# Post-layernorm transformer layer on 8 cores: the projection's cast moves from GpSimd to ScalarE, and the layer-norm finish is queued one group earlier

## The reference

```python
q = (x @ q_w.T + q_b).reshape(b, s, 16, 128)
k = x @ k_w.T + k_b
v = x @ v_w.T + v_b
scores = einsum('bqhd,bkd->bhqk', q, k) / 128 ** 0.5      # causal mask, softmax
out = einsum('bhqk,bkd->bqhd', attn, v).reshape(b, s, 2048)
x = _layernorm(x + out @ o_w.T + o_b)
x = _layernorm(x + einsum('bsi,oi->bso', x, weight * scale_weight[:, None]) + bias)
# _layernorm: (x - mean) / sqrt(var + 1e-5)
```

## Time and profile before

| what | us |
|---|---|
| runs shown: median (lowest, highest) of 2 | 2372.36 (2342.03, 2402.69) |
| profiled execution, its own time | 2288.15 |
| its span, slowest core (core 3) | 2286.6 |
| spans of the eight cores | 2271.2 to 2286.6 |
| closing stage in that span | 1538.8 to 2286.6 |

### The profile page before, as it was taken

The page is one execution under the profiler, slowest core; times in us unless marked ns, Lnnn a source line. Parts: engine busy times, 40 slices in busy tenths (PEclk is TensorE's granted clock), DMA queues, the critical chain, the costliest instruction groups (busy, mean ns, idle before and its releaser), DMA issues.

```text
span 2286.6 us, 26159 instructions; the slowest of 8 cores (2271.2 to 2286.6 us)
## 1 busy us (share of the span) xinstructions
PE 1545.0 (68%) x7216; PEld 671.9 (29%) x7216; DVE 919.3 (40%) x1985; ACT 906.9 (40%) x2270; POOL 384.0 (17%) x399
## 2 busy tenths in 40 slices
PE   0899963445555566666566666669879595989773
PEld 0344421222222222222223332333323232333221
DVE  0000003445555555555555555540626415166234
ACT  0112114655555565666555555551123320123311
POOL 0000020000000000000000000007646244675331
PEclk9999985666766667777577677679989798999886
DMA  9222289800000000000000000006543346553252
GB/s 146 39 38 43 41 101 110 112 1 1 1 1 1 1 1 1 1 1 1 1 1 1 1 1 1 1 15 184 152 111 129 101 137 160 172 167 103 75 154 92
DMA packets 43640, 137.06 MB, mean 60 GB/s; under 512 B 5835, under 2 KB 5868, under 8 KB 42988
## 3 DMA queue, kind: packets, MB, share of 16 engines
q1 hardware_dynamic: 28988, 84.02, 12.1%
q0 software_dynamic: 5296, 34.60, 11.4%
q10 hardware_dynamic: 9216, 16.78, 2.6%
HBM read 153.21 MB, written 33.55 MB: 82 GB/s over the span
## 4 chain that ended last, share of the span: by engine, by line
PE 43%; DVE 15%; ACT 15%; issue 13%; DMA 9%; another core or an unknown queue 3%; POOL 1%; DVEq 1%; ACTq 0%; SPq 0%; POOLq 0%
ACT expS L396 12%; PE psT L259 10%; DVE mpart L375 8%; PE psT L836 4%; PE psT L770 4%; PE psS L484 3%; DMA outT<-outb 3%; DMA wost<-wo_bf 3%; PE psU L836 3%; PE psS L347 2%; PE psO L836 2%; PE psU L770 2%; DMA trib_s<-tri 2%; DVE expST L458 2%
## 5 line engine op out<-in xcount | busy, mean ns | idle before, releaser
L375 DVE TENSOR_REDUCE mpart<-psS 128x1 f32<-128x512 f32 (+3 forms) x327 | 190.3, 600 | 374.1 <-PE psS L356 368.0
L797 POOL TENSOR_TENSOR ycs<-yscr,xres 128x512 f32<-128x512 f32 x64 | 85.6, 1337 | 1319.3 <-ACT yscr L786 1288.8
L396 ACT ACTIVATE expS<-psS,negm 128x512 bf16<-128x512 f32 (+3 forms) x327 | 201.6, 619 | 216.5 <-DVE negm L379 215.6
L259 PE MATMUL psT<-xTbf,qwst 128*128 128x512 bf16 x1024 | 221.2, 379 | 0.2 <-ACT Vsb L241 0.2
L439 PE MATMUL psS<-diagP,expS 128*128 128x128 bf16 x1075 | 137.3, 264 | 98.1 <-ACT expS L396 58.7
L408 DVE TENSOR_REDUCE den<-dpart 128x1 f32<-128x2 f32 (+2 forms) x192 | 29.9, 156 | 414.5 <-ACT expS L396 414.5
L347 PE MATMUL psS<-KT,QTO 128*128 128x512 bf16 (+3 forms) x327 | 147.2, 475 | 70.0 <-ACT expS L396 56.5
L484 PE MATMUL psS<-expST,Vsb 128*128 128x512 bf16 x320 | 130.8, 555 | 83.8 <-ACT expST L463 59.0
L836 PE MATMUL psT<-x1T,fwst 128*128 128x512 bf16 x512 | 130.1, 414 | 51.5 <-DMA fwst<-fw_bf 28.5
L417 ACT ACTIVATE diagP<-ident_s,rcp 128x128 bf16<-128x128 bf16 x256 | 102.9, 402 | 144.4 <-DVE rcp L413 144.4
L770 PE MATMUL psT<-QTO,wost 128*128 128x512 bf16 x512 | 122.4, 396 | 22.0 <-DMA wost<-wo_bf 20.9
(11 more groups left out here) (111 smaller groups left out, 2590.2 us busy)
## 6 DMA issues: line engine op xcount, KB each, us to landing
wost<-wo_bf SPq DMA_DIRECT2D x64, 512.0 KB, 4.5
fwst<-fw_bf SPq DMA_DIRECT2D x64, 512.0 KB, 3.4
xres<-xT ACTq DMA_DIRECT2D x64, 256.0 KB, 4.7
outT<-outb SPq DMA_DIRECT2D x64, 256.0 KB, 3.2
xTbf<-xT POOLq DMA_DIRECT2D x1, 8192.0 KB, 58.8
qwst<-qw POOLq DMA_DIRECT2D x16, 512.0 KB, 6.2
wo_bf<-wo POOLq DMA_DIRECT2D x4, 2048.0 KB, 82.1
fw_bf<-fw POOLq DMA_DIRECT2D x4, 2048.0 KB, 101.0
```

What stands on the lines that cost most here:

```text
L259: e.matmul(bk[:], qwst[:, (ot % 2) * D + dt * 128: (ot % 2) * D + dt * 128 + 128], xTbf[:, dt * S + c * W: dt * S + c * W + W], start=(dt ...
L375: mc=mcol + kc: e.reduce_max(mpart[:, mc:mc + 1], slot[:, 0:wdt], axis=AX.X),
L396: e.activation(expS8[:, (par * 4 + qt % 4) * S + kc * W: (par * 4 + qt % 4) * S + kc * W + wdt], slot[:, 0:wdt], AF.Exp, bias=negm8[:, nco ...
L797: pbuf=pbuf: e.tensor_tensor(pbuf[:, ot * W:(ot + 1) * W], yscr[:, (ot % 2) * W:(ot % 2) * W + W], xres[:, (ot % 3) * W:(ot % 3) * W + W], ...
```

## The change

Two edits. First, the bf16 cast of an O group goes from POOL to ACT; the square stays on POOL. Second, in both kinds of tail the step `emit_lnfin` joins the step of the last statistics, so that it and all steps behind it are queued one group earlier.

```diff
@@ o_group
-                    E_castO[c][ot] = p.op("gpsimd", lambda e, ot=ot, ysl=ysl,
-                                          pbuf=pbuf: e.tensor_copy(
+                    E_castO[c][ot] = p.op("scalar", lambda e, ot=ot, ysl=ysl,
+                                          pbuf=pbuf: e.copy(
                         castsc[:, ysl * W:(ysl + 1) * W],
-                        pbuf[:, ot * W:(ot + 1) * W]), waits=wcs, inc="p")
+                        pbuf[:, ot * W:(ot + 1) * W]), waits=wcs, inc="a")
@@ make_tail, kind "O"
                                      emit_stats("O", c, 14),
-                                     emit_stats("O", c, 15)),
-                            lambda: emit_lnfin("O", c),
+                                     emit_stats("O", c, 15),
+                                     emit_lnfin("O", c)),
                             lambda: emit_bcast_a("O", c),
@@ make_tail, kind "F"
                             lambda: (emit_stats("F", c, 14),
-                                     emit_stats("F", c, 15)),
-                            lambda: emit_lnfin("F", c),
+                                     emit_stats("F", c, 15),
+                                     emit_lnfin("F", c)),
                             lambda: emit_bcast_a("F", c),
```

## The result

The changed kernel takes 1.0213 times the time of the kernel before (95% interval 1.0185 to 1.0241). The medians over all runs are 2339.12 us (11 runs, 2329.06 to 2382.19) and 2291.58 us (10 runs). So it lost 47.5 us. Some executions of either kernel are slow, with a die at a lower granted clock; the ratio is made without them, from medians of 2335.79 and 2286.99 us, which makes 48.8 us. The two runs that were shown ahead of the prediction are the longest of the ten. Forecast were 50 us on top of the profiled execution, which makes 2338, and 2422 us on top of the median of the two runs shown.

What follows compares the result with a forecast made beforehand. PE was read as holding 43% of the chain, DVE, ACT, DMA waits and issue gaps the rest. O blocks +70.7 and layer-norm finish -21 gave about +50 us, on the shown runs' median 2372.36: 2422 us, range 2320 to 2470.

Steps and rivals of the forecast that it cites:

- The ring: In O (attention projection) blocks, residual load, add and cast dispatch follow one another, 13 rounds a block from group 3: +70.7 us.
- P = 5.7 us: Time of one round in the O blocks: X plus 1.5 us for add and hand-overs.
- X = 4.2: Residual load's time in the O blocks, from issue to landing, in us; ends taken as 3.1 and 6.1.
- Block by block: Cast on ACT priced for each O block: O0 +17.8, O1 +16.3, O2 +13.9, O3 +22.7, sum +70.7 us.
- The first waits about 0.2 us: At O1's start, with the layer-norm finish moved earlier, the first broadcast waits about 0.2 us; the same 1.2 us shift in O3.
- F blocks: FFN blocks, layer-norm finish one group earlier: F0 and F2 -5 us each, F1 and F3 -5.5 each, -21 in all.
- what is predicted is that median plus 50: Whole kernel: +50 us put on 2372.36, the median of the runs shown, making 2422 us.
- Short rounds: Rival, O blocks: residual loads come down to 3.1 to 3.6 us; 0 to 1% slower; chance 0.32.
- No ring: Rival, O blocks: ACT's sequencer issues the load past the waiting cast; -21 us, 2267, 0.9% faster; chance 0.04.
- hidden rounds: Rival, O blocks: a round is no longer than PE's 4.1 us; 2271, 0.7% faster; chance 0.03.
- long rounds: Rival, O blocks: X stays at 4.7 to 6.1 us; +74 to +141 us, 3 to 6% slower; chance 0.14.

Runs made afterwards that it cites:

- tails-only kernel: Against the kernel before, only the layer-norm finish is queued one group earlier, in O and F tails; the cast stays on POOL. Ratio 0.9935.
- best version: Kernel before with finish moved up in F blocks only, x1T copies queued inside O1 and O3, outputs two tiles per group behind weight loads; 0.9803, retaken 0.9706 (2230.25 us).

## Why the prediction was right, and where not

- **The ring.** Right, and shown from three sides: it is there in the trace, it goes when only the issue is moved (ahead of the cast, or to SP), and it comes back without any cast when the load is made to wait. It makes 50.5 of the 68.2 us; nearly all of the rest is the cast on ACT at the ends and the starts of the blocks (16.5 us).
- **P = 5.7 us, X = 4.2.** The mean over eight cores of X was 3.83, 4.01, 4.06 and 3.88 us in O0, O1, O2 and O3, and the issues were 5.40, 5.64, 7.18 and 5.61 us apart (O2 is paced by the outputs for half its length). X was 0.1 to 0.4 too high, P up to 0.3. X so came out below 4.1 us, where the prediction's own sum puts the loss under 2%: with the measured X it gives +37 us, and 46.3 were measured in this stage. The rest was not priced: a round was X plus 1.57 to 1.73 us instead of 1.5, and the ring began 13.3, 18.6 and 18.3 us into O0, O1 and O3 instead of 12.8, 17.7 and 17.0. That the whole comes so near to +50 is in part luck. The fit of the Trainium skill ("DMA: Bandwidth & Descriptors", section "Anatomy of one DMA") would have made 2.6 us of X, an estimate; that section gives it for DMAs issued from GpSimd, and these are issued from ACT. No load of the ring came under 2.96.
- **Block by block** (mean over the cores): O0 +14.2 for +17.8 forecast, O1 +17.8 for +16.3, O2 +14.4 for +13.9, O3 +21.7 for +22.7; together +68.2 for +70.7. On core 3, from whose rows the forecast was worked out, it is +13.9, +21.4, +9.0 and +25.4, together +69.7. The rounds are shorter than forecast, and the broadcast's wait was not priced, and the two cancel in part.
- **"The first waits about 0.2 us"** was mis-sized. PE waits 2.67 us in O1, and the next group takes 5.31 us instead of 3.63, at a mean granted clock of 0.68. The finish is over 7.2 us after the block's start (1621.27 to 1628.48, and 1966.77 to 1973.96 in O3 of the tails-only kernel). A wait of 0.2 us would need a first group of 7 us; it took 4.54 us in the first place and 3.63 in the second. In O2 and O3 of the tails-only kernel the blocks are 4.6 us longer for it.
- **F blocks.** -5.5 and -4.7 for -5 each (F0, F2), -4.3 and -7.4 for -5.5 each (F1, F3). Right, and -21.9 for -21 in all. In F1 of core 3 the first output's issue came 9 us earlier in the block, as worked out, but the weight load behind the last output took 6.01 us instead of 4.
- **What failed is the base of the absolute time.** The step was "what is predicted is that median plus 50": 2422 us. The two runs shown had a median of 2372.36 and were the longest of ten; over the ten it is 2291.58, 3 us from the profiled execution. The +50 us had been worked out from the rows of that execution, and so belong on its time. The sum made against the profiled execution, 2338, is 1 us from the 2339.12 measured. Of the 83 us by which 2422 is off, 81 are the base and 2 the sum.
- **The rivals.** Short rounds are out by the ratio's interval: up to +21 us would be 1.009, and it begins at 1.0185. Their reason was half right, as the loads did get faster in the ring (3.83 to 4.06 us in the mean of a block, 4.59 to 5.37 before), but not down to 3.6. No ring and hidden rounds are out by the trace; long rounds too, since X stayed under 4.7.

## What to carry to other kernels

In these traces a DMA issue on a compute engine's queue is held up like any other instruction of that engine: before you put a waiting operation on that engine, look which issue comes behind it, and whether its wait leads back to the load before. If it does, the buffers no longer count, and the load's whole latency goes into every round; issue the load ahead of the operation that waits. Price a moved step against each place where it runs, since the same edit took some 5 us off each F block and put 4.6 on O2 and O3. And a difference that was read from a profiled execution is added to that execution's own time, above all when few runs are at hand.

## What the runs showed of the hardware that I had not expected

A load that is issued late and more alone is faster, yet the block slower (O0, mean over the cores): 3.83 us and 84.7 us behind the cast, 4.91 us and 69.2 us on SP.

In both profiles of the best version two cores ran a stretch at a lower granted clock than the rest. The first profile, the window 1618 to 1690, core 6 and then core 3 (columns as in the windows above, PEclk the third from the end):

```profile
1618.00:1690.00 72.00, 70.09 (x254) 24.63 (x253) 37.87 (x36) 18.78 (x32) 47.22 (x42) 0.82 0.63 151
```

```profile
1618.00:1690.00 72.00, 64.06 (x276) 24.34 (x274) 40.57 (x36) 20.62 (x34) 53.91 (x48) 1.00 0.58 165
```

Sixteen matmuls took 4.37 us there instead of 3.63, for some 160 us. It was cores 6 and 7 (0.82 in this window) in the first profile and cores 0 and 1 (0.79 from 2000 to 2060) in the second, where cores 2 and 3 had 0.94 and 0.97. The Trainium skill ("TensorE: Matmul & The Clock Gate", section "Seeing it yourself") tells of a limiter that takes a whole die to 13/16, which is 0.81, once three of its cores run dense matmuls. The level agrees, the reach does not: cores 4 and 5, on one die with 6 and 7, stayed at 1.00 and 0.98. In the one profile of the kernel before, the four cores that I looked at had 0.97 to 1.00 in such stretches. It is not this version's alone, though: in one timed execution of the kernel before, cores 4 and 5 had a mean granted clock of 0.789 and 0.786 and spans of 2316.9 and 2309.4 us, the other six 0.795 to 0.804 and at most 2286.2 us. What brings it about was not tried.
